# Eight-core transformer layer: the V projection planned into the layernorm phase, Q/K weights loaded a head ahead, and one pair of ternary steps reordered

## The reference

```python
xn = layernorm(x)                      # x: 4 x 4096 x 2048, f32
q, k, v = xn @ Wq + bq, xn @ Wk + bk, xn @ Wv + bv   # 16 heads of 128
q, k = rope(q), rope(k)
a = softmax(q @ k.T / sqrt(128))       # over all 4096 keys
o = (a * tril) @ v                     # mask applied after the softmax
h = square(relu(xn @ ternarize(w_fc).T))             # 5120 wide
out = x + (o @ Wo + bo) + h @ ternarize(w_proj).T
# ternarize(w) = mean|w| * sign(w) where |w| > 0.7 mean|w|, else 0
```

## Time and profile before

| | us |
|---|---|
| median of 3 runs shown | 5248.44 |
| lowest and highest | 5242.32 and 5531.73 |
| the profiled execution | 5242.52 |
| its span (core 5, the slowest of 5202.0 to 5241.0) | 5241.0 |
| TensorE matmul busy in it | 3876.7 (74%) |
| layernorm and V projection | 0 to 910 |
| attention | 910 to 3640 |
| up-projection | 3640 to 4307 |
| down-projection, output projection | 4307 to 5241 |

### The profile page before, as it was taken

One profiled execution on the slowest core, in us unless ns is written; L12 is line 12 of the kernel. 1 busy time (PEld: TensorE's weight loads), 2 busy tenths in 40 slices (PEclk: granted clock), 3 DMA queues, 4 the chain that ended last, 5 costly groups with the idle time before them and its releaser, 6 DMA issues.

```text
span 5241.0 us, 66567 instructions; the slowest of 8 cores (5202.0 to 5241.0 us)
## 1 busy us (share of the span) xinstructions
PE 3876.7 (74%) x23892; PEld 2316.4 (44%) x23892; DVE 1215.0 (23%) x1858; ACT 1549.7 (30%) x2017; POOL 714.9 (14%) x1234
## 2 busy tenths in 40 slices
PE   0019888777777776777677777776988879889698
PEld 0017777544554444544444445444433334344233
DVE  2222111222222222321121112212444430000011
ACT  3430000433443334443454345444333320000000
POOL 0002222000001010010000000000444430000000
PEclk9569899999999999999999999998999989999899
DMA  8772222122212222122212221222555547666665
GB/s 179 194 170 59 46 47 52 52 57 56 62 52 59 58 57 64 50 56 57 59 50 56 55 59 50 57 55 83 201 193 190 194 173 254 217 232 216 172 162 152
DMA packets 304729, 564.40 MB, mean 108 GB/s; under 512 B 162336, under 2 KB 195104, under 8 KB 281120
## 3 DMA queue, kind: packets, MB, share of 16 engines
q1 hardware_dynamic: 163872, 367.13, 23.0%
q0 software_dynamic: 140544, 193.02, 15.4%
HBM read 434.21 MB, written 117.44 MB: 105 GB/s over the span
## 4 chain that ended last, share of the span: by engine, by line
PE 56%; DMA 14%; ACT 9%; issue 8%; DVE 7%; POOL 3%; SPq 2%; DVEq 0%; another core or an unknown queue 0%; ACTq 0%; POOLq 0%
PE psum L1091 10%; PE psum L724 9%; PE psum L377 7%; PE psum L682 7%; PE psum L990 6%; ACT expT L705 5%; PE psum L761 5%; PE psum L600 5%; PE psum L1182 4%; DMA qsw_b<-qe_b 3%; PE psum L540 3%; DMA x_t<-xp 2%; DMA wqk_q<-wq 2%; DMA hT_tc<-hT_scr 2%; POOL hT_scr L1026 2%
## 5 line engine op out<-in xcount | busy, mean ns | idle before, releaser
L705 ACT ACTIVATE expT<-psum 128x1024 bf16<-128x1024 f32 x1024 | 982.2, 1028 | 643.0 <-PE psum L761 588.3
L682 PE MATMUL psum<-qrotT,krotT 128*128 128x256 bf16 x4096 | 619.3, 284 | 412.6 <-ACT expT L705 295.9
L377 PE MATMUL psum<-wv_sl,xnT 128*128 128x256 bf16 x4096 | 470.7, 279 | 428.5 <-DVE v_ev L390 248.4
L990 PE MATMUL psum<-xnT,qfc 128*128 128x512 bf16 x2560 | 575.5, 388 | 84.7 <-DVE qfc L977 83.9
L682 PEld LDWEIGHTS psum<-qrotT,krotT 128*128 128x128 bf16 x4096 | 367.0, 100 | 602.3 <-issue 551.6
L377 PEld LDWEIGHTS psum<-wv_sl,xnT 128*128 128x128 bf16 x4096 | 407.7, 100 | 492.2 <-issue 436.8
L1091 PE MATMUL psum<-qpr,hT_tc 128*128 128x512 bf16 x2560 | 559.9, 382 | 67.8 <-DMA hT_tc<-hT_scr 66.5
L724 PE MATMUL psum<-expT,ones_cb 128*128 128x256 bf16 x4096 | 524.3, 285 | 0.0
L600 PE MATMUL psum<-xnT,wqk_k 128*128 128x512 bf16 x2048 | 450.0, 379 | 23.4 <-ACT qe_b L613 12.9
L724 PEld LDWEIGHTS psum<-expT,ones_cb 128*128 128x128 bf16 x4096 | 418.7, 102 | 65.8
L990 PEld LDWEIGHTS psum<-xnT,qfc 128*128 128x128 bf16 x2560 | 253.2, 100 | 406.6 <-issue 122.6
(11 more groups left out here) (83 smaller groups left out, 2204.8 us busy)
## 6 DMA issues: line engine op xcount, KB each, us to landing
hT_tc<-hT_scr SPq DMA_DIRECT2D x32, 2560.0 KB, 11.1
stb<-wfcT SPq DMA_DIRECT2D x160, 256.0 KB, 2.7
stb<-wprT SPq DMA_DIRECT2D x160, 256.0 KB, 2.7
wpr_b<-wprT SPq DMA_DIRECT2D x40, 1024.0 KB, 5.2
wfc_b<-wfc SPq DMA_DIRECT2D x40, 1024.0 KB, 7.2
x_t<-xp SPq DMA_DIRECT2D x32, 1024.0 KB, 8.6
qsw_b<-qe_b POOLq DMA_DIRECT2D x192, 128.0 KB, 2.3
qpr_scr<-qprs POOLq DMA_DIRECT2D x160, 128.0 KB, 2.2
```

The source lines that it names most:

```text
L377: ins = t.matmul(psum[:, bank:bank+256], xnT[:, cb*T + tb*128: cb*T + (tb+1)*128], wv_sl[dch % 2][:, cb*256:(cb+1)*256], start=(cb == 0), ...
L682: ins = t.matmul(psum[:, reg+pos*256: reg+pos*256+256], krotT[:, kb*128:(kb+1)*128], qrotT[:, c*W:(c+1)*W], start=(pos % 2 == 0), stop=(po ...
L705: s.activation(expT[:, g0*W:(g0+4)*W], psum[:, reg:reg+1024], AF.Exp, scale=SCALE).then_inc(sem_s, 1)
L990: ins = t.matmul(psum[:, reg + tc*512: reg + (tc+1)*512], qfc[fb % 2][:, cb*128:(cb+1)*128], xnT[:, cb*T + tc*512: cb*T + (tc+1)*512], sta ...
```

## The change

Stage 1: `Wv` is laid out on the host as `wvr`, one contiguous 16 KB row of f32 for each partition and slice. The V projection is no longer emitted after layernorm. `plan_v(tb)` is called after each layernorm block and emits loads, matmul blocks, evictions and stores up to targets worked out from `tb`; what is left is emitted afterwards by `plan_v(999)`. The order of the blocks is now by quarter of rows first, then slice, then the 8 row blocks of the quarter, so each slice of Wv is loaded four times, 32 loads in all, each used for 8 blocks. There are four PSUM banks, four `v_ev` tiles and four store semaphores instead of two. ScalarE's squares go to PSUM columns 2048 to 4095 instead of the tile `dump`, which is gone.

Stage 2: the loads of `wqk_q` and `wqk_k` for head h+1 are emitted within head h after chunk 1 of its 8, not at the start of head h+1.

Stage 3: `emit_wpr_strip(fb)` is called after the ternary steps of the w_fc strip of the same `fb`, not before its load.

```diff
     wprT = np.ascontiguousarray(wpr.T)
+    wvr = np.ascontiguousarray(Wv.reshape(16, 128, 8, 256).transpose(2, 1, 0, 3)
+                               .reshape(8, 128, 4096))
...
             xn_t = [E1(nc.sbuf_tensor(f"xn_t{i}", [128, H], BF16)) for i in range(2)]
...
-            v_ev = [E1(nc.sbuf_tensor(f"v_ev{i}", [128, 256], BF16)) for i in range(2)]
+            v_ev = [E1(nc.sbuf_tensor(f"v_ev{i}", [128, 256], BF16)) for i in range(4)]
...
+            def plan_wv_load(li):
+                dch = li % 8
+                buf = wv_sl[li % 2]
+                war = wv_last_mm[li - 2] if li >= 2 else None
...
+                def f(g, dch=dch, buf=buf, war=war, swvc=swvc):
                     if war is not None:
                         g.wait_ge(sem_t, war)
...
+                    g.dma_start(out=buf[:], in_=d["wvr"][dch]).then_inc(swvc.sem, 16)
                 em("gpsimd", f)
                 wv_load.append((swvc.sem, swvc.inc()))
...
+            def plan_v_mm(idx):
+                sw, rem = idx // 64, idx % 64
+                dch, t8 = rem // 8, rem % 8
+                tb = 8 * sw + t8
+                li = idx // 8
+                bank = (idx % 4) * 512
+                lw = wv_load[li]
+                qrd = xnq_ready[sw]
+                war = vproj_ev[idx - 4] if idx >= 4 else None
+                def f(t, li=li, tb=tb, bank=bank, lw=lw, qrd=qrd, war=war):
+                    t.wait_ge(*lw)
+                    t.wait_ge(*qrd)
+                    if war is not None:
+                        t.wait_ge(sem_v, war)
...
+                if idx % 8 == 7:
+                    wv_last_mm.append(vproj_mm[-1])
+
+            def plan_v_ev(idx):
+                dch = (idx % 64) // 8
+                bank = (idx % 4) * 512
+                mmw = vproj_mm[idx]
+                war = v_store[idx - 4] if idx >= 4 else None
+                svc = svst[idx % 4]
+                def f(v, dch=dch, bank=bank, idx=idx, mmw=mmw, war=war, svc=svc):
+                    v.wait_ge(sem_t, mmw)
+                    v.wait_ge(sem_v, bvb_ready)
+                    if war is not None:
+                        v.wait_ge(svc.sem, war)
+                    v.tensor_tensor(v_ev[idx % 4][:], psum[:, bank:bank+256],
+                                    bvb[:, dch*256:(dch+1)*256], ALU.add).then_inc(sem_v, 1)
+                em("vector", f)
+                vproj_ev.append(sv.inc())
...
+            def plan_v_st(idx):
...
+                evw = vproj_ev[idx]
+                svc = svst[idx % 4]
+                def f(g, dch=dch, tb=tb, idx=idx, evw=evw, svc=svc):
+                    g.wait_ge(sem_v, evw)
+                    g.dma_start(out=d["v_scr"][tb*128:(tb+1)*128, dch*256:(dch+1)*256],
+                                in_=v_ev[idx % 4][:]).then_inc(svc.sem, 16)
+                em("gpsimd", f)
+                v_store.append(svc.inc())
+
+            vp = {"ld": 2, "mm": 0, "ev": 0, "st": 0}
+            NV = 4 * 64
+            def plan_v(tb):
+                qdone = min((tb + 1) // 8, 4)
+                tmm = min(64 * qdone, max(0, int((tb - 9) * 6.3)))
+                tev = max(0, int((tb - 10) * 6.3))
+                tld = min(32, 2 + max(0, int((tb - 8) * 0.85)))
+                while True:
+                    did = False
+                    if vp["ld"] < tld and len(wv_last_mm) >= vp["ld"] - 1:
+                        plan_wv_load(vp["ld"]); vp["ld"] += 1; did = True
+                    if vp["mm"] < tmm:
+                        idx = vp["mm"]
+                        if idx // 8 < len(wv_load) and (idx < 4 or idx - 4 < len(vproj_ev)):
+                            plan_v_mm(idx); vp["mm"] += 1; did = True
+                    if (vp["ev"] < min(tev, len(vproj_mm))
+                            and (vp["ev"] < 4 or vp["ev"] - 4 < len(v_store))):
+                        plan_v_ev(vp["ev"]); vp["ev"] += 1; did = True
+                    if vp["st"] < len(vproj_ev):
+                        plan_v_st(vp["st"]); vp["st"] += 1; did = True
+                    if not did:
+                        break
 
             sl = d["wq"][:, 0:128].rearrange("(cb p) n -> p cb n", p=128)
             def f(g, sl=sl):
...
-                    s.activation(dump[:], buf[:], AF.Square,
+                    if tb == 0:
+                        s.wait_ge(sem_v, bvb_ready)
+                    s.activation(psum[:, 2048:4096], buf[:], AF.Square,
                                  accum_out=sumsq[:, tb:tb+1]).then_inc(sem_s, 1)
...
                     xnq_ready.append((sxq.sem, sxq.n))
+                plan_v(tb)
 
             xnT_ready = list(xnq_ready)
 
...
+            while vp["mm"] < NV or vp["ev"] < NV or vp["st"] < NV or vp["ld"] < 32:
+                plan_v(999)
+            v_ready = tuple((c.sem, c.n) for c in svst)
...
-                    sl = d["wq"][:, h*128:(h+1)*128].rearrange("(cb p) n -> p cb n", p=128)
-                    def f(g, sl=sl, prev=prev):
-                        g.wait_ge(sem_t, prev["qproj_mm"])
...
+                    mil["wq_ld"], mil["wk_ld"] = PENDING_WQK[h]
...
+                        sl = d["wq"][:, (h+1)*128:(h+2)*128].rearrange(
+                            "(cb p) n -> p cb n", p=128)
+                        qpw = mil["qproj_mm"]
+                        def f(g, sl=sl, qpw=qpw):
+                            g.wait_ge(sem_t, qpw)
+                            g.dma_start(out=wqk_q[:].rearrange("p (cb n) -> p cb n", n=128),
+                                        in_=sl).then_inc(swq.sem, 16)
+                        em("gpsimd", f)
+                        wqv = swq.inc()
+                        sl = d["wk"][:, (h+1)*128:(h+2)*128].rearrange(
+                            "(cb p) n -> p cb n", p=128)
+                        kpw = mil["kproj_mm"]
+                        def f(g, sl=sl, kpw=kpw):
+                            g.wait_ge(sem_t, kpw)
+                            g.dma_start(out=wqk_k[:].rearrange("p (cb n) -> p cb n", n=128),
+                                        in_=sl).then_inc(swk.sem, 16)
+                        em("gpsimd", f)
+                        PENDING_WQK[h+1] = (wqv, swk.inc())
                 emit_p2(NCH-1)
                 while RQ:
                     emit_stat_red(RQ.pop(0))
...
             fc_ld, fc_tern, fc_mm, fc_relu, fc_sq, fc_st = [], [], [], [], [], []
             for fb in range(NFB):
-                emit_wpr_strip(fb)
                 sl = d["wfc3"][fb]
                 war = fc_tern[fb-2] if fb >= 2 else None
...
                                            gtb[:], ALU.is_lt, ALU.subtract).then_inc(sem_v, 1)
                 em("vector", f)
                 fc_tern.append(sv.inc())
+                emit_wpr_strip(fb)
                 reg = (fb % 2) * 2048
```

87 lines of the change are left out of this document (22 added, 65 removed).

## The result

The changed kernel takes 4882 to 4891 us where the one before takes 5242 to 5248: a ratio of 0.9317, 95% interval 0.9303 to 0.9331, or some 358 us less. The prediction was 4820 us, 428 less: the direction and two of the three parts came out, the first part was put too high.

The account below looks back on a forecast made before the run. TensorE's waits in the V projection, Q projection and up-projection were taken as the bound; 5241.0 - 168 - 160 - 100 = 4813 us of span, predicted 4820 us. Range 4735 to 4900, the forecast's own 4750 to 4875.

Parts of the forecast that it names:

- the first part: Stage 1, V projection woven into layernorm: attention starts at 742 instead of 910.42 us, 168 us less; bounds 114 to 249.
- The period of one layernorm block: Stage 1, time per layernorm block while V blocks are woven in: worked out as 14.4 us, taken as 14.
- The stall of a load: Stage 1, TensorE's wait per Wv load: 1.3 us with DMA otherwise quiet, 4.3 us beside layernorm.
- The signs of being wrong: Reduces every 11 or 17 us, seams past 55 us, or a head's first swap landing after 12.5 us.
- a load beside the transposes: Stage 1, seams between layernorm quarters: 5 us added to the 43.0 us seam for a Wv load.
- part 2: Q projection, wq and wk loaded one head early: 15 x 10.7 = 160 us less; bounds 100 to 174.
- The lower one: Stage 1, lower bound of the woven layernorm period: 11.05 us, TensorE never waiting; this part then gains 249 us.
- The DMA floor of 11.4: Stage 1, DMA engine work per layernorm block from layernorm traffic, Wv loads and V stores: 11.4 us.
- The upper one: Stage 1, upper bound of the woven layernorm period: 17 us, the load slowed by 6 us more; gain 114 us.
- layernorm starves: Stage 1 rival, chance 0.16: loads slow transposes and x_t, periods of 17 us; 4874 us, to 4900 with longer seams.
- The layout at nothing: Stage 1, Wv's new long rows: load landing kept at 9.0 us, no gain counted for the layout.
- Part 3: Up-projection, qfc loaded ahead of qprs: stall and low clock go, 96.7 plus 3.7, 100 us less; bounds 74 to 101.

## Why the prediction was right and where it was wrong

**The period of one layernorm block: wrong, and nearly the whole miss comes from it.** The prediction worked out 14.4 us, took 14, and 16.3 was measured. It followed one load of Wv, its 9 us, the V stores behind it, four tiles of cover. That is the arrangement of the kernel with the `xn_scr` store from SyncE, where only loads are in GpSimd's queue beside the V stores, and there 15.1 us was measured. So the miss of 2.3 us has two parts of about the same size. The stall of a load was put too low: 14 for 15.1. And 1.3 us more come from the other transfer that GpSimd issues in the same stretch, which the prediction never followed, the `xn_scr` store: once per layernorm block, 0.5 MB, with an `x_t` load issued at the same moment. The prediction did count its bytes ("I add 3 us of it to the load", and 5.0 us of the DMA engines per block), but not its place ahead of three or four V stores on GpSimd. By its own rule, that a small transfer behind loads lands with them, this was to be seen in the order of `em` calls: store of `xn_t`, then `plan_v(tb)`.

What that made, on core 0: block 16 at 246 for 240 (though its block 11 came at 131.7, 7 us before the 139.09 taken), block 24 at 411 for 384, the last of the 132 woven evictions done at 539 for 494, attention at 798 for 742. That is 6 + 21 + 18 + 11 = 56 us. The last 11 lie behind the layernorm, where eight V blocks take 15.9 us at the median for the 15.3 worked out, and up to 23.1 in the first groups. This shows the stall of a load with the DMA otherwise quiet: 1.9 us, where 1.3 was worked out.

**The signs of being wrong.** The prediction named three. The periods came nearer to the 17 than to the 14. The first seam passed 55 us on two of eight cores (60.9 and 59.7, in the profiled execution), so what the sum took for a load beside the transposes, 5 us, holds on the five with 47 to 49 alone. The third sign, the swap, is under part 2.

**The bounds.** The lower one, 11.05 us, is reached in single quarters, with eight tiles (11.2) and with both transfers away (11.0). The DMA floor of 11.4 was put slightly too high: with eight tiles the engines are 0.90 to 0.97 busy between seams on the six cores with periods of 11.2 to 11.4, which is 10.3 to 11.0 us per block. The case that the prediction set against this part ("put wholly on the path, 24 x 6.6 = 158 us would eat nearly all of this part") didn't come true; the extra loads' bytes cost little once they were covered. The upper one, 17, held (one quarter of one core had 17.2), and with it the range of 4735 to 4900; the forecast's own range, 4750 to 4875, was missed. The rival "layernorm starves" gave 4874 and is the nearest to 4885, by its number. That its number came so near is luck. Its reason was slower transposes and `x_t`, but the `x_t` loads land no later than before (8.1 us at the median for 8.6), and clearly longer seams are there on three of eight cores and in the first seam alone: that doesn't explain the periods.

**The layout at nothing: wrong in size.** The new rows land in 9.2 us at the median on core 0 (9.0 taken), in 9.4 beside the layernorm, but the old ones land in 10.1 to 11.3, and undoing the layout costs 25 us. The formula of "Anatomy of one DMA" (the Trainium skill) gave an estimated 6.8 us; the quickest of the 32 on core 0 took 8.4.

**Part 2: right.** 165.2 measured, of which 3.7 belong to the first strip of the up-projection, against 160. TensorE passes from the last matmul of a head to the Q projection without a gap, `v_head` is late next and the swap behind it (core 0, timeline at the first change of heads):

```profile
953.63 13.98 PE L574 MATMUL psum<-xnT,wqk_q 128*128 128x512 bf16 x64
...
956.17 1.70 POOL L551 DMA_DIRECT2D v_head<-v_scr  x1 [0.70 <-issue]
962.06 0.53 POOL L596 DMA_DIRECT2D qsw_b<-qe_b  x1 [4.19 <-ACT qe_b L587]
962.59 0.53 POOL L597 DMA_DIRECT2D qsw_b<-qe_b  x1
966.19 0.69 DVE L605 TENSOR_TENSOR rt<-qe_b,cos_s 128x1024 bf16<-128x1024 bf16 x1 [11.79 <-DMA qsw_b<-qe_b]
```

The second swap lands at 966.1, 12.5 us after the head's first matmul, where the text had 12.0 and set the sign of being wrong at 12.5. Over the 15 changes of heads on eight cores it is 12.0 at the median and 11.1 to 13.6 in all, over 12.5 in 19 of 120; so the size is right and the sign was set too close to it. `v_head` lands in 9.4 us at the median (9.9 taken), which is about 965.6 here, and the swap right behind it.

**Part 3: right.** 95.3 measured, 96.7 worked out; the wait for `qfc` is 10.7 us in all ("under 12"), the granted clock is 1.00 from 3400 to 3900 us and the matmuls take 216 ns each there (500 us for 2319), 213.9 taken.

**Squaring into PSUM: right to cost it at nothing.** The activation takes 1.86 us into PSUM, 1.91 into the tile that it had before.

## What to carry to other kernels

When small stores are woven in among large transfers, list everything that the issuing engine puts into its queue in that stretch, not only the transfers that the change adds; each large one can be a stall of its own for the small ones behind it, also because the engine issues in order. Give the small stores' source buffers enough depth to cover the landing time of the largest transfer that may be under way, instead of trying to make them land sooner: here four more tiles of 64 KB brought 140 us, while another queue brought 70 and another issuer for the store ahead brought 25. And where two causes of a stall overlap, removing one shows only a part of their common cost (here a quarter or a third), so test them one by one and together.

## What the runs showed of the hardware

- A 64 KB store lands in 1.8 to 1.9 us at the median where it runs alone (the kernel before). In the woven quarters the medians of the cores are 2.9 to 3.5 us beside a 1 MB load and a 0.5 MB store of another queue (up to 9.2), 5.6 to 5.9 where GpSimd issues the 0.5 MB store ahead of it (up to 8.9), 4.2 to 6.3 where 2 MB loads that cast to bf16 run but that store is in another queue, and 6.6 to 7.0 with both.
- A 2 MB load of Wv issued beside the 16 transposes of a seam landed in 9 to 10 us on most cores and in 22.4 and 22.5 on two, and the seam took 47 to 49 us and 60.9 and 59.7. The same pairs come in other kernels: 19.7 us and a seam of 57.0 with eight tiles, 29.9 and 67.1 with the store from SyncE as well. Without loads the seams were 40 to 43 us.
- TensorE's granted clock in the woven stretch was 0.85 and 0.87 on core 0 (246 to 363 and 411 to 523 us), against 0.50 while it stood still in a seam (222 to 242 us) and 1.00 in the up-projection, where it never paused. The V matmuls took 493.2 us where they took 470.7 before, so the stalls cost a little clock as well as their own time.
- With eight tiles the DMA engines were busy 0.83 to 0.97 of 246 to 300 us on the eight cores (210 to 260 GB/s each), and TensorE still set the pace: its granted clock was 1.00 on six of them, and 0.93 and 0.94 on the two with the lower shares, where it paused more (busy 47.39 and 50.04 of 54 us).
